# Graph attention and a routed expert layer on one core: TensorE's attention slots and expert steps as loops, and the scaled sums of a batch finished in one piece

## The reference

```python
x = x + gnn(layernorm(x), adj, W, a)
x = x + ffn(layernorm(x), Wg, bg, W1, b1, W2, b2)

# gnn: 4 heads of 32
h = x @ W;  s1 = h . a1;  s2 = h . a2
e = leaky_relu(s1[:, None] + s2[None, :], 0.2), -inf where adj == 0
out = softmax(e) @ h

# ffn: 8 experts, each row goes to the best 2 by gate score
p, experts = softmax(top_k(x @ Wg.T + bg, 2))
out += p_e * (relu(x @ W1[e].T + b1[e]) @ W2[e].T + b2[e])
```

## Time and profile before

| | |
|---|---|
| time, median of 3 runs | 625.65 us (623.48 to 626.25) |
| time of the profiled execution | 624.53 us |
| its span (first to last instruction) | 622.6 us |
| TensorE busy | 477.3 us (77%), 7450 matmuls |
| TensorE weight loads busy | 435.4 us (70%), 7509 |
| VectorE busy | 515.9 us (83%), 1619 instructions |
| ScalarE busy | 447.7 us (72%), 908 |
| GpSimd busy | 402.5 us (65%), 342 |
| mean granted TensorE clock | 0.928 of full |

### The profile page before, as it was taken

The page is one execution under the profiler, slowest core; times in us unless marked ns, Lnnn a source line. Parts: engine busy times, 40 slices in busy tenths (PEclk is TensorE's granted clock), DMA queues, the critical chain, the costliest instruction groups (busy, mean ns, idle before and its releaser), DMA issues.

```text
span 622.6 us, 22344 instructions
## 1 busy us (share of the span) xinstructions
PE 477.3 (77%) x7450; PEld 435.4 (70%) x7509; DVE 515.9 (83%) x1619; ACT 447.7 (72%) x908; POOL 402.5 (65%) x342
## 2 busy tenths in 40 slices
PE   0687887977888787988867866799999999997000
PEld 0576787867888777988766755688888888887000
DVE  4689998999999999999988984678788888886297
ACT  1585778878888888998717745678888888884264
POOL 2241235887777777787776787878778887887300
PEclk9997999889989999999896998999999999999555
DMA  8922221222222233231113252233333323331499
GB/s 312 399 107 68 70 70 34 73 98 96 95 75 64 93 106 99 96 100 37 37 45 83 76 147 78 79 90 89 88 88 93 88 79 91 86 86 37 136 367 307
DMA packets 60781, 67.92 MB, mean 109 GB/s; under 512 B 7267, under 2 KB 46318, under 8 KB 60417
## 3 DMA queue, kind: packets, MB, share of 16 engines
q1 hardware_dynamic: 41936, 44.31, 22.9%
q0 software_dynamic: 8816, 17.46, 8.4%
q10 hardware_dynamic: 9920, 4.73, 2.6%
HBM read 44.16 MB, written 23.22 MB: 108 GB/s over the span
## 4 chain that ended last, share of the span: by engine, by line
issue 31%; DVE 29%; POOL 15%; PE 9%; DMA 8%; ACT 6%; POOLq 1%; SPq 1%; DVEq 0%; ACTq 0%
POOL expert_out L519 13%; PE bank L1369 4%; DVE edge L816 4%; DVE bs L719 3%; ACT xn L575 3%; DVE G L824 3%; DMA G<-in_L_ffn_W 2%; PE bank L1360 2%; DVE mv L722 2%; DMA adji<-expert_out 2%; POOL expert_rows L469 2%; DVE T L833 2%; DVE rowt L863 1%; DVE sc L759 1%; DMA G<-expert_out 1%
## 5 line engine op out<-in xcount | busy, mean ns | idle before, releaser
L519 POOL DMA_INDIRECT expert_out<-late,bidx x142 | 170.1, 1198 | 43.3 <-issue 42.7
L469 POOL DMA_INDIRECT expert_rows<-rowt,idx x128 | 156.6, 1223 | 40.6 <-issue 35.7
L570 ACT ACTIVATE G<-bank,s2c 128x512 uint8<-128x512 f32 x256 | 153.7, 703 | 0.0
L673 ACT ACTIVATE late<-bank,b1s,sc 128x256 f32<-128x256 f32 x284 | 137.3, 563 | 13.0 <-PE bank L1543 12.5
L1369 PE MATMUL bank<-V,G 128*128 128x66 bf16 x3072 | 131.1, 198 | 4.0 <-ACT G L570 0.5
L1369 PEld LDWEIGHTS bank<-V,G 128*128 128x128 fp8e4 x3072 | 121.0, 100 | 8.8 <-issue 1.6
L1560 PE MATMUL bank<-W2h,G 128*128 x1704 | 107.6, 220 | 20.2 <-DVE late L1239 18.7
L1560 PEld LDWEIGHTS bank<-W2h,G 128*128 128x128 f16 x1704 | 97.4, 98 | 36.2 <-issue 35.8
L1543 PE MATMUL bank<-late,W1h 128*128 128x256 f16 x852 | 107.1, 277 | 0.0
L1224 DVE TENSOR_TENSOR G<-late,G 128x1024 f16<-128x1024 f32 x71 | 87.0, 1226 | 2.4
L1543 PEld LDWEIGHTS bank<-late,W1h 128*128 x852 | 81.6, 99 | 9.1
(11 more groups left out here) (166 smaller groups left out, 688.9 us busy)
## 6 DMA issues: line engine op xcount, KB each, us to landing
adji<-in_adj SPq DMA_DIRECT2D x16, 1024.0 KB
V<-expert_rows SPq DMA_DIRECT2D x71, 130.0 KB
adji<-expert_out SPq DMA_DIRECT2D x8, 512.0 KB, 5.8
G<-expert_out SPq DMA_DIRECT2D x8, 512.0 KB, 8.4
expert_out<-late,bidx POOLq DMA_INDIRECT x142
G<-in_L_ffn_W SPq DMA_DIRECT2D x1, 2048.0 KB, 13.4
late<-in_L_ffn_W SPq DMA_DIRECT2D x1, 2048.0 KB, 10.1
expert_rows<-rowt,idx POOLq DMA_INDIRECT x128
```

Source lines behind the costliest of these rows:

```text
L469: pool.indirect_dma_start(xs, bass.IndirectOffsetOnAxis(ap=idx[:, Z.q, k, j:j + 1], axis=0), rowt[:, Z.q, j, :], None).then_inc(scattered[ ...
L519: pool.indirect_dma_start(ybuf, bass.IndirectOffsetOnAxis(ap=bidx[:, B.o, t:t + 1], axis=0), ysb[:, B.q, t, :], None, bounds_check=2 * TOK ...
L570: act.activation(Gs[:, M.p, h // 2, mt, :, h % 2], zb[h][:, :], ACT.Sign, bias=s2c[:, M.p, mt, h:h + 1]).then_inc(S["z_used"], 1)
L673: act.activation(h32[:, U.p, c, :], Up[U.p][c // 2][:, (c % 2) * BLK:(c % 2 + 1) * BLK], ACT.Relu, bias=b1s[:, bass.ds(ex * NC + c, 1)], s ...
```

## The change

It does three things.

1. **TensorE's attention slots 6 to 15 are a loop** (`pe.Fori`) of five turns with two slots each. Slots 0 to 5, 16 and 17 stay written out. In the loop a batch number is a register's value, so the value that a wait compares with is computed at run time.
2. **TensorE's expert steps 17 to 64 are a loop** of six turns with eight steps each (`UNROLL = 8`, `LOOPS = 6`). Registers of one turn aren't carried into the next, so the first step of a turn (`at.first`), and the first step behind the loop, read the expert numbers of three more blocks. The wait for the second part of the table (`tab_ready` 2) moves from step 38 to the front of the loop.
3. **VectorE finishes the scaled sums once for a batch.** `residual` and `attention` work on all four fourths at once; the calls for the first half at the top of a slot are gone, and both calls of `stats2` stand where the second stood. `scaled_sums` 0 now also waits for the last `attention`, which stands ahead of it on the same engine.

```diff
+LOOP_STEP = SHARED + 1
+UNROLL = 8
+LOOPS = (BLOCKS - 3 - LOOP_STEP) // UNROLL
+LOOP_SLOT = 6
...
+        def looped_step(u, i):
+            at = lambda k: Batch(LOOP_STEP + u + k, i, UNROLL)
+            at.first = u == 0
+            return at
...
-            def residual(R, half):
-
-                ts = slice(2 * half, 2 * half + 2)
-                dve.wait_ge(S["t_steps"], R.n * NT + 2 * half + 2)
-                dve.tensor_tensor(T[:, ts, :, 0, :], T[:, ts, :, 0, :], T[:, ts, :, 1, :], ALU.subtract) \
+            def residual(R):
+
+                dve.wait_ge(S["t_steps"], R.n * NT + NT)
+                dve.tensor_tensor(T[:, :, :, 0, :], T[:, :, :, 0, :], T[:, :, :, 1, :], ALU.subtract) \
                    .then_inc(S["sum_ready"], 1)
...
-                c.did(dve.reciprocal(rec[:, ts, :], T[:, ts, :, 0, HD]))
+                dve.wait_ge(S["sum_ready"], R.n + 1)
+                ge(dve, S["x1_ready"], R.n)
+                c.did(dve.reciprocal(rec[:, :, :], T[:, :, :, 0, HD]))
                 c.wait()
                 c.did(dve.tensor_tensor(
-                    att[:, ts, :].rearrange("p t (h d) -> p t h d", d=HD), T[:, ts, :, 0, 0:HD],
-                    rec[:, ts, :].unsqueeze(3).to_broadcast([P, 2, H, HD]), ALU.mult))
+                    att[:, :, :].rearrange("p t (h d) -> p t h d", d=HD), T[:, :, :, 0, 0:HD],
+                    rec[:, :, :].unsqueeze(3).to_broadcast([P, NT, H, HD]), ALU.mult))
                 if tail(R):
                     c.wait()
-                    xh = xr[:, R.n * NT + 2 * half:R.n * NT + 2 * half + 2, :]
-                    dve.tensor_tensor(xh, xh, att[:, ts, :], ALU.add).then_inc(S["x1_ready"], 1)
+                    xh = xr[:, R.n * NT:(R.n + 1) * NT, :]
+                    dve.tensor_tensor(xh, xh, att[:, :, :], ALU.add).then_inc(S["x1_ready"], 1)
...
-                if m2:
-                    residual(m2, 0)
                 if m4:
                     route(m4, 8)
                 if m3:
                     shift2(m3)
-                if m2:
-                    attention(m2, 0)
...
-                if m2:
-                    stats2(m2, 0)
...
                 if m2:
+                    stats2(m2, 0)
                     stats2(m2, 1)
...
-            slots(pe, body, 0, NB + 2)
+            for n in range(LOOP_SLOT):
+                body(at_slot(n))
+            with pe.Fori(0, (NB - LOOP_SLOT) // 2) as i:
+                body(at_slot(LOOP_SLOT, i))
+                body(at_slot(LOOP_SLOT + 1, i))
+            for n in range(NB, NB + 2):
+                body(at_slot(n))
...
-                ey, ex = held[0], held[2]
+                ey, ex = held[0], expert(U) if at.first else held[2]
...
-                if X and X.n == FULL:
-                    pe.wait_ge(S["tab_ready"], 2)
+                if at.first:
+                    ey = expert(Y)
+                    held[1:] = [expert(at(1)), ex]
                 held[:] = held[1:] + [expert(X) if X else None]
...
-            for n in range(3, BLOCKS):
+            for n in range(3, LOOP_STEP):
                 layers(step(n))
+            pe.wait_ge(S["tab_ready"], 2)
+            with pe.Fori(0, LOOPS) as i:
+                for u in range(UNROLL):
+                    layers(looped_step(u, i))
+            for n in range(LOOP_STEP + LOOPS * UNROLL, BLOCKS):
+                layers(step(n, n == LOOP_STEP + LOOPS * UNROLL))
```

More of the change, by code:

```diff
@@ L311, in XTp @@
         def XTp(B):
-            return XTb[1 if B.n < SHARED else B.p]
+            return XTb[1 if isinstance(B.n, int) and B.n < SHARED else B.p]
         def Yp(B):
-            return Yb[1 if B.n < SHARED else B.p]
+            return Yb[1 if isinstance(B.n, int) and B.n < SHARED else B.p]
         names = """ld_const ld_small ld_w1 ld_w2 ld_x0 ld_x1 ld_x2 ld_adj0 ld_adj1
@@ L354, in blocks, with step, is_block, early @@
                 body(Batch(n))
-        def step(n):
-            return lambda k: Batch(n + k) if 0 <= n + k < BLOCKS else None
+        def step(n, first=False):
+            at = lambda k: Batch(n + k) if 0 <= n + k < BLOCKS else None
+            at.first = first
+            return at
+        def looped_step(u, i):
+            at = lambda k: Batch(LOOP_STEP + u + k, i, UNROLL)
+            at.first = u == 0
+            return at
+        def is_block(B, n):
+            return isinstance(B.n, int) and B.n == n
+        def early(B):
+            return isinstance(B.n, int) and B.n < SHARED
         def pad_rows(eng, experts):
@@ L477, in low_rows, with add @@
                     .then_inc(S["lo_ready"], 1)
[L479 to L482, removed]
+            def add(R):
+                hold(pool, S["att_steps"], R.n * ATT_STEPS + ATT_STEPS, S["pool_turns"])
+                xh = xr[:, R.n * NT:(R.n + 1) * NT, :]
+                pool.tensor_tensor(xh, xh, att[:, :, :], ALU.add).then_inc(S["x1_ready"], 1)
             def body(at):
@@ L497, in body @@
                     scatter(m4, 1)
-                if m1 and not tail(m1):
-                    add(m1, 0)
                 if m4:
@@ L503, in body @@
                 if m1 and not tail(m1):
-                    add(m1, 1)
+                    add(m1)
             hold(pool, S["ld_const"], 16, S["pool_turns"])
@@ L869, in stats2 @@
                 c.k = 4 * half
-                hold(dve, S["x1_ready"], R.n * 2 + half + 1, S["dve_turns"])
+                hold(dve, S["x1_ready"], R.n + 1, S["dve_turns"])
                 if half == 0:
@@ L1148, in body @@
                 if m2:
-                    residual(m2, 1)
+                    residual(m2)
                 if p0:
@@ L1154, in body @@
                 if m2:
-                    attention(m2, 1)
+                    attention(m2)
                 if m4:
@@ L1254, in _ @@
             route(b13, 12)
-            residual(b15, 1)
+            residual(b15)
             positions(b13)
-            attention(b15, 1)
+            attention(b15)
             chosen(b13)
@@ L1508, in body, with at_slot @@
                     weight_rows()
-            slots(pe, body, 0, NB + 2)
+            def at_slot(n, i=None):
+                if i is None:
+                    at = lambda k: Batch(n + k) if 0 <= n + k < NB else None
+                    at.s = n
+                else:
+                    at = lambda k: Batch(n + k, i)
+                    at.s = None
+                return at
+            for n in range(LOOP_SLOT):
[5 more added lines that the diff above has]
+                body(at_slot(n))
             held = [None, None, None]
@@ L1520, in layers @@
                     pe.wait_ge(ld_rows[X.q], X.f * 16 + 16)
-                    ge(pe, S["xt_ready"], X.n if X.n < SHARED else X.n - 1)
-                    if X.n == 0:
+                    ge(pe, S["xt_ready"], X.n if early(X) else X.n - 1)
+                    if is_block(X, 0):
                         pe.wait_ge(S["v_steps"], NB * X_STEPS)
-                    if X.n == SHARED:
+                    if is_block(X, SHARED):
                         pe.wait_ge(S["xn2T_ready"], NB)
```

22 lines of the change are left out of this document (9 added, 13 removed).

## The result

The changed kernel takes 659.91 us, the median of 4 runs (659.6 to 661.92), against 625.0 us for the kernel before (4 runs). The ratio is 1.0567, with a 95% interval of 1.0533 to 1.0600: 35 us slower. A ratio compares, for each kernel, only its executions within 1.5% of its quickest, so where times scatter it can differ from the quotient of the medians. The profiled execution took 659.6 us, its span 657.8.

What follows compares the result with a forecast made beforehand. VectorE was taken to bound attention and TensorE's sequencer the expert stage. 624.5 - 8 + 11.8 + 16.8 + 1.8 - 2.4 = 644.5, predicted as 645 us; own range 636 to 654, wide range 631 to about 676.

Steps and rivals of the forecast that it cites:

- the halves: VectorE in attention: merging both halves' residual and attention work saves 0.6 us a slot, -8 us, between -10 and -4.
- the rival of fetches: TensorE's loops: each taken jump stops it about 3 us to fetch instructions; time 669 us, chance 0.35.
- Does a new wait eat it?: VectorE's attention slot: moving stats2 adds no wait; the 0.84 us of room before the gate scores stays.
- VectorE as busy as before: Sign of being right, attention: VectorE's busy share is unchanged while slots get 0.6 us shorter outside the jumps.
- The slot loop: TensorE's attention slots 6 to 15: 24 register instructions a slot and the jump are hidden; 0, up to +5 us.
- The expert steps: TensorE's expert loop: extra instructions in 42 steps cost +11.8 us, extra work in six first steps +16.8 us.
- s: Extra time of each expert-loop step that isn't first in its turn, from three more instructions: 0.28 us.
- F: Extra time of a turn's first expert step, for three further loads, computed addresses and waits, and the branch: 2.8 us.
- Behind the loop: TensorE's first expert step after the loop reads three expert numbers again: +1.8 us.
- Given back: End of the expert stage: a slower TensorE lets GpSimd catch up on its sends, -2.4 us.
- GpSimd sets the expert stage: Rival, expert stage: GpSimd's sends set the pace, hiding TensorE's slower sequencer; 616 us, chance 0.07.
- The signs of being wrong: Loop steps staying at 3.0 us, or attention not over 4 us shorter with VectorE idle at scores or masks.

Runs made afterwards that it cites:

- The whole edit: Kernel before with VectorE's part of the change alone (both stats2 where the second stood), TensorE's loops written out: 627.6 us, ratio 1.0047.
- the two kernels of that length: Kernel before with only the expert loop, in turns of sixteen: 648.3 us; changed kernel with first stats2 early and turns of sixteen: 738.6 us, ratio 1.0293.

## Why the prediction was right, and where it was not

659.9 us lies inside 631 to 676 and outside the forecast's own 636 to 654. The sum was 15 us low: 11 of them are the halves (+2.9 for -8), 5 the expert loop (32.9 for 30.4 - 2.4). That the time lies inside the wide range is in part luck: its upper end was set by the rival of fetches, which did not happen, and the halves were forecast with the opposite sign.

- **What bounds.** Right for both stages: VectorE full in attention, TensorE's sequencer in the expert stage (three further loads in straight code lengthened their step from 3.05 to 5.11 us).
- **The halves, -8 us.** The term that failed. The work does shrink, and the kernel with `stats2` left early shows -5.9; its edge operation is still longer than before (1592 to 1457 ns, 16 x 0.135 = 2.2 us), so 8 of saving less 2.2 gives what was measured. The whole edit gives +2.9. The step that failed is "Does a new wait eat it?": I counted the 0.78 us of statistics that leave the stretch only as room for the gate scores. They were also the cover under which GpSimd's subtraction ran (its start at 232.38 and the earlier trace rows would have shown it), and without it the edge operation stands still 0.8 us longer. That is no wait on a semaphore: it appears in no list of waits, only as a longer duration. "VectorE as busy as before" held, and I took it for a sign of health.
- **The slot loop, 0.** Right: 0.9996. Taken jumps and registers are both hidden.
- **The expert steps.** s 0.32 for 0.28 and F 2.9 for 2.8. For 42 steps and six turns 13.4 + 17.4 where I said 28.6. The gap before the down matmuls in a first step was 1.98 us for "over 2". I was right to take the pace of the earlier trace rows and not the recorded lengths, which gave 16 with the loads behind the loop.
- **Behind the loop, +1.8.** One set of loads costs 2.1.
- **Given back, -2.4.** The last down result is at 612.3 and the last send at 617.7: 5.4 us for 7.9, -2.5. The 32.9 us of the expert loop alone are a difference of whole times and have this in them already: in its trace the steps from step 17 to the last take 186.1 us where they took 151.9, 34.2 more, for 30.4 forecast.
- **The rival of fetches**, chance 0.35. It did not happen in this kernel: 0.21 us a jump, and no packet of q8 in the expert loop. By the Trainium skill ("Runtime: NRT & Kernel Launch", Instruction fetch mechanics) a taken branch out of a two-page window must fetch; the trace disagrees for TensorE with bodies of 856 and some 1,240 records. The same section gives TensorE room for 2,048 instructions, with which these two agree. But jumps that fetch exist, and at 1,698 records, below that figure too, they showed once, at 4.4 to 5.1 us a jump, more than the 3 I priced. What decides between the two kernels of that length (where the body lies, or the chip) is not settled.
- **GpSimd sets the expert stage**, 616 us: refuted by 659.9, and GpSimd now waits 32 us for results.
- **The signs of being wrong.** Attention was not shorter by 4 us, but the sign asked for an idle VectorE as well, and VectorE was busy standing still. Steps of 3.35 us in the loop and the gap in every first step came as forecast.

## What to carry to other kernels

An instruction that is moved can be worth more for where it stood than for what it costs: before moving one on VectorE, look at what GpSimd does at that moment, and which of VectorE's operations behind it have both inputs in SBUF or, as the edge operation here, stood still beside GpSimd. A growing mean duration of an operation that the diff does not touch is the sign of it, and no list of waits shows it. For a loop on an engine whose sequencer is full, count register instructions at their pace (0.1 us each, an expert number 0.7), not at their recorded length, and look at the jump's duration and the instruction queue's packets in a turn before trusting a longer body.

## What was not expected of the hardware

- GpSimd's 1.94 us subtraction adds nearly its whole overlap to VectorE's edge operation (0.57 us of overlap: +0.46; 1.34: +1.22), and a 0.18 us comparison of two buffers became 1.27 us; reductions and statistics beside it keep their time (274 ns for 280). GpSimd stands still in the same way: a piece of 264 columns that started 0.02 us behind the edge operation took 1.68 us instead of 0.62.
- TensorE's loops of 856 and some 1,240 records jumped in 0.21 to 0.24 us, with no instruction transfer in the former and one in the latter's four turns; one of 1,698 jumped in 0.22 to 0.24 us in one kernel, and took 4.4 to 5.1 us with nine transfers a turn in another.
- The same kernel took 624 us on two chips and 718 on a third, at a mean granted clock of 0.88 instead of 0.93. Whether the clock has a part in it isn't shown; TensorE's sequencer pauses there in straight code.
